# Moving the destination and weight arithmetic of a routed tile ahead in a mixture-of-experts stage, with four-deep buffers for its results

## The reference

```python
logits = jnp.einsum('bsd,de->bse', x, Wr) * SCALE
_, idx = jax.lax.top_k(logits + rb, K)                  # K = 2 of E = 8
w = jax.nn.softmax(jnp.take_along_axis(logits, idx, axis=-1), axis=-1)
...
h = jnp.einsum('bsd,edh->bseh', x, W1) * jax.nn.silu(jnp.einsum('bsd,edh->bseh', x, W3))
expert_out = jnp.einsum('bseh,ehd->bsed', h, W2)        # H = 512
out = jnp.einsum('bsed,bse->bsd', expert_out, w_full)
hs = jnp.einsum('bsd,dh->bsh', x, Ws1) * jax.nn.silu(jnp.einsum('bsd,dh->bsh', x, Ws3))
out = out + jnp.einsum('bsh,hd->bsd', hs, Ws2)
```

## Time and profile before

| | us |
|---|---|
| median of three runs | 3486.91 |
| the profiled execution | 3485.83 |
| its span | 3483.7 |
| shared-expert units, as a stretch | 2744 to 2856 |
| routed units, first and last turn of rows | 2859.5 and 3409.0 |

### The profile page before, as it was taken

One profiled execution on the slowest core, in us unless ns is written; L12 is line 12 of the kernel. 1 busy time (PEld: TensorE's weight loads), 2 busy tenths in 40 slices (PEclk: granted clock), 3 DMA queues, 4 the chain that ended last, 5 costly groups with the idle time before them and its releaser, 6 DMA issues. The chain is left out here.

```text
span 3483.7 us, 52943 instructions
## 1 busy us (share of the span) xinstructions
PE 2999.7 (86%) x17256; PEld 2171.2 (62%) x17256; DVE 2530.5 (73%) x3858; ACT 1449.3 (42%) x2076; POOL 1674.7 (48%) x1186
## 2 busy tenths in 40 slices
PE   6999999698889889889898898988987897777773
PEld 4888888555546545555554554554554897777773
DVE  3555545687897897888888779878877647766666
ACT  2222222354445445445445444544543333333333
POOL 2222222265574565566557556655654343444445
PEclk9999999899999999999999999999998998888886
DMA  8000100200100100100100100100101324444445
GB/s 236 13 14 14 22 18 13 55 25 16 41 25 19 44 19 25 44 13 25 44 18 19 50 13 19 53 15 20 49 13 59 110 71 143 146 144 147 143 138 177
DMA packets 137039, 197.69 MB, mean 57 GB/s; under 512 B 16992, under 2 KB 96864, under 8 KB 136736
## 3 DMA queue, kind: packets, MB, share of 16 engines
q1 hardware_dynamic: 115696, 160.52, 15.7%
q10 hardware_dynamic: 14224, 14.58, 1.6%
q0 software_dynamic: 6816, 18.75, 1.4%
HBM read 118.54 MB, written 41.71 MB: 46 GB/s over the span
## 5 line engine op out<-in xcount | busy, mean ns | idle before, releaser
L1082 ACT ACTIVATE raw<-b_ps 128x1024 f32<-128x1024 f32 x512 | 505.4, 1021 | 460.6 <-PE b_ps L854 385.6
L1226 DVE TENSOR_SCALAR raw<-raw 128x1024 f32<-128x1024 f32 x512 | 578.2, 1135 | 117.5 <-ACT raw L1082 115.5
L965 PE MATMUL b_ps<-raw 128*64 128x512 f32 x2048 | 510.2, 620 | 113.9 <-DVE raw L1226 113.2
L853 PE MATMUL b_ps<-b_QQ,b_KT 128*128 128x512 f32 x1024 | 436.7, 426 | 15.6 <-DMA b_QQ<-b_QQ 8.6
L823 POOL TENSOR_TENSOR b_acc<-b_acc,raw 128x512 f32<-128x512 f32 x256 | 373.0, 1457 | 86.1 <-DVE raw L1226 54.2
L854 PE MATMUL b_ps<-b_QQ,b_KT 128*128 128x512 f32 x1024 | 407.0, 397 | 0.0
L827 POOL TENSOR_TENSOR b_acc<-b_acc,raw 128x512 f32<-128x512 f32 x256 | 388.7, 1518 | 20.1
L806 POOL TENSOR_TENSOR b_QQ<-raw,b_QQ 128x512 fp32r<-128x512 f32 x128 | 165.3, 1291 | 404.5 <-ACT b_QQ L1032 404.5
L1678 PE MATMUL c_ps<-c_xT_l,c_w_h 128*128 128x256 f32 x1504 | 359.1, 322 | 0.0
L965 PEld LDWEIGHTS b_ps<-raw 128*64 128x64 f32 x2048 | 126.3, 138 | 371.2 <-issue 196.8
L853 PEld LDWEIGHTS b_ps<-b_QQ,b_KT 128*128 128x128 f32 x1024 | 195.2, 191 | 247.8 <-issue 188.5
(11 more groups left out here) (262 smaller groups left out, 7268.5 us busy)
## 6 DMA issues: line engine op xcount, KB each, us to landing
c_raw<-in_L_ffn_W_dram SPq DMA_DIRECT2D x117, 512.0 KB, 5.4
b_QQ<-b_QQ SPq DMA_DIRECT2D x128, 256.0 KB, 3.7
xs<-zeros ACTq DMA_DIRECT2D x1, 10140.0 KB, 67.9
c_xg<-xs SPq DMA_DIRECT2D x39, 260.0 KB, 2.7
b_rows<-in_ctx_dram SPq DMA_DIRECT2D x9, 1024.0 KB, 7.5
a_xt<-in_x_dram SPq DMA_DIRECT2D x72, 64.0 KB, 2.2
b_rows<-x SPq DMA_DIRECT2D x9, 512.0 KB, 7.1
x<-a_x1t SPq DMA_DIRECT2D x64, 64.0 KB, 1.9
```

Source lines behind the costliest of these rows:

```text
L853: pe.matmul(bank(key, a), k, QQ[:, n % 2, hh, 0, :], start=True, stop=False)
L965: mm = pe.matmul(bank(key)[hh * HD:(hh + 1) * HD, :], V[:, t, (2 * p + hh) * HD:(2 * p + hh + 1) * HD], probs[:, at_step(j, hh), (t % 2) * ...
L1082: ins = act.activation(probs[:, at_step(j, hh), :], both(key), ACT.Exp, scale=SCALE)
L1226: dve.tensor_scalar(pr, pr, HI, LO, ALU.min, ALU.max).then_inc(clipped, 1)
```

## The change

The instructions of `goals` are issued elsewhere and in other forms:

- In the list of VectorE `goals(u + 1 - DENSE)`, for the next unit, stands behind `lo(u, 0)`; `goals(u - DENSE)` at the end of the unit is gone. SyncE's list is not edited.
- `share` and `goal_u` are four deep. `goals(j)` waits for the sends of tile j - 4, and `take` now waits for the sends of tile j - 2, whose `yr` it overwrites.
- The two `tensor_scalar` instructions become `scalar_tensor_tensor` with a second operand in SBUF, for which there are two new constant tiles, `nought` and `second_at`, that GpSimd fills at the start of the stage. There are eight instructions as before, in another order, with two `link`s in place of three. `goals_ready` is signalled by the one that writes `goal_u`.
- The counts on `consts` go up by two.

```diff
-        share = sb("c_share", [P, 2, 3, TT])
+        share = sb("c_share", [P, 4, 3, TT])
         goal = sb("c_goal", [P, 4, TT])
+        nought = sb("c_nought", [P, TT])
+        second_at = sb("c_second_at", [P, TT])
...
-        goal_u = sb("c_goal_u", [P, 2, TT], U32)
+        goal_u = sb("c_goal_u", [P, 4, TT], U32)
...
+                pool.memset(nought[:, :], 0.0).then_inc(consts, 1)
+                pool.memset(second_at[:, :], float(SECOND)).then_inc(consts, 1)
...
-                            out=ys[:, :], out_offset=bass.IndirectOffsetOnAxis(ap=goal_u[:, j % 2, t:t + 1], axis=0),
+                            out=ys[:, :], out_offset=bass.IndirectOffsetOnAxis(ap=goal_u[:, j % 4, t:t + 1], axis=0),
...
                 def goals(j):
 
-                    k = j % 2
+                    k, q = j % 2, j % 4
                     dve.wait_ge(xg_in[k], 16 * (j // 2 + 1))
-                    if j >= 2:
-                        dve.wait_ge(sent[k], 16 * TT * (j // 2))
+                    if j >= 4:
+                        dve.wait_ge(sent[k], 16 * TT * (j // 2 - 1))
                     own = owner[:, j:j + 1]
-
-                    link(dve.tensor_scalar(goal[:, 2, :], hole[:, :], float(j * T), None, ALU.add))
                     eid, token = xg[:, k, :, EID], xg[:, k, :, TOKEN]
-                    dve.scalar_tensor_tensor(share[:, k, 0, :], eid, own, xg[:, k, :, SHARE], ALU.is_equal, ALU.mult)
-                    dve.scalar_tensor_tensor(share[:, k, 1, :], eid, own, xg[:, k, :, SHARE + 1], ALU.not_equal, ALU.mult)
-                    dve.tensor_scalar(goal[:, 0, :], eid, own, float(SECOND), ALU.not_equal, ALU.mult)
-                    link(dve.scalar_tensor_tensor(goal[:, 1, :], token, 0.0, goal[:, 2, :], ALU.is_equal, ALU.mult))
+
+                    dve.scalar_tensor_tensor(goal[:, 2, :], hole[:, :], float(j * T), nought[:, :], ALU.add, ALU.add)
+                    dve.scalar_tensor_tensor(goal[:, 0, :], eid, own, second_at[:, :], ALU.not_equal, ALU.mult)
+                    dve.scalar_tensor_tensor(share[:, q, 0, :], eid, own, xg[:, k, :, SHARE], ALU.is_equal, ALU.mult)
+                    link(dve.scalar_tensor_tensor(share[:, q, 1, :], eid, own, xg[:, k, :, SHARE + 1], ALU.not_equal, ALU.mult))
+                    dve.scalar_tensor_tensor(goal[:, 1, :], token, 0.0, goal[:, 2, :], ALU.is_equal, ALU.mult)
+                    dve.tensor_tensor(share[:, q, 2, :], share[:, q, 0, :], share[:, q, 1, :], ALU.add)
                     link(dve.tensor_tensor(goal[:, 3, :], goal[:, 0, :], token, ALU.add))
-                    dve.tensor_tensor(goal_u[:, k, :], goal[:, 3, :], goal[:, 1, :], ALU.add)
-                    dve.tensor_tensor(share[:, k, 2, :], share[:, k, 0, :], share[:, k, 1, :], ALU.add).then_inc(goals_ready, 1)
+                    dve.tensor_tensor(goal_u[:, q, :], goal[:, 3, :], goal[:, 1, :], ALU.add).then_inc(goals_ready, 1)
...
                         dve.wait_ge(goals_ready, j + 1)
+                        if j >= 2:
+                            dve.wait_ge(sent[j % 2], 16 * TT * (j // 2))
                         for t in range(TT):
                             ins = dve.tensor_scalar(yr[:, j % 2, t, :], src[:, t * D:(t + 1) * D],
-                                                    share[:, j % 2, 2, t:t + 1], None, ALU.mult)
+                                                    share[:, j % 4, 2, t:t + 1], None, ALU.mult)
...
                     lo(u, 0)
+                    if nxt:
+                        goals(u + 1 - DENSE)
                     if u == 0:
                         places()
                     if u >= DENSE:
                         split_lo(weight_set(u), 2)
                     product(u, 1)
                     lo(u, 1)
-                    if u >= DENSE:
-                        goals(u - DENSE)
```

More of the change, by code:

```diff
@@ L1535, in _ @@
                 pool.memset(every_f[:, :], 1.0).then_inc(consts, 1)
-                pool.wait_ge(consts, 8)
+                pool.wait_ge(consts, 10)
                 pool.tensor_copy(lane[:, :], step_u[:, :]).then_inc(consts, 1)
-                pool.wait_ge(consts, 9)
+                pool.wait_ge(consts, 11)
                 pool.tensor_scalar(steps[:, :], lane[:, :], float(T), None, ALU.mult).then_inc(consts, 1)
@@ L1547, in _ @@
                 pool.tensor_copy(wrs[:, :, 0, :], wr[:, :, :]).then_inc(consts, 1)
-                pool.wait_ge(consts, 16)
+                pool.wait_ge(consts, 18)
                 pool.tensor_tensor(wrs[:, :, 1, :], wr[:, :, :], wrs[:, :, 0, :].bitcast(F32), ALU.subtract
@@ L1616, in logits @@
                     if c == 0:
-                        pe.wait_ge(consts, 17)
+                        pe.wait_ge(consts, 19)
                     else:
@@ L1833, in _ @@
                     link(tops(c))
-                dve.wait_ge(consts, 17)
+                dve.wait_ge(consts, 19)
                 dve.tensor_copy(y[:, :, EID], topi[:, :, 0])
```

## The result

The changed kernel took 3292.59 us (median of four runs, 3288.86 to 3295.84); the kernel before, 3486.72 us on the same chip. The ratio is 0.9443, with a 95% interval of 0.9426 to 0.9459: 194 us less. The profiled execution took 3288.86 us, its span is 3287.0 us. The kernel after is 2 us slower there and the kernel before 7 us faster, so the size of the gain is known to some 10 us.

What follows compares the result with a forecast made beforehand. Row loads waiting for goals bound the routed loop at 14.65 us a turn; VectorE at 9.49 would follow. 37 turns plus 6.7 for add_dense make 357.8 instead of 542.1; with the ends -186.7, so 3300 us, range 3274 to 3352.

Steps and rivals of the forecast that it cites:

- What bounded before: Routed units: the next row load waits for goals, then turn and first product follow; 37 turns of 14.65 us.
- What is late next: Routed units after the change: VectorE's loop sums to 9.49 us a turn, 0.4 above TensorE's 9.07.
- The rule beside it: VectorE instructions with two SBUF inputs contend with GpSimd's SBUF reads; whichever issues first holds the shared pair throughout.
- Rival B: VectorE's L1828 loses the lock to GpSimd's second split: 1.28 us more a turn, +47 us, 3347; chance 0.18 with lower clock.
- add_dense: In eight units, standing ahead of take, it moves the 3.86 us wait by 0.84: 6.7 us in all.
- goals(1): Now issued in unit 16, it costs its 1.1 us once.
- The end: Last unit, lo(53, 1) to the last take: about 9.6 us instead of 13.1, 3.5 less.
- Row loads: SyncE's burst of weights and rows, needing some 5.5 us, comes 13 us ahead of the turn: costed at nothing.
- `sent` in `goals`: goals(j) waits for send(j-4): 8.7 us of room against landings of 5.6 (median) and 8.3 (longest); no wait.
- Rival D: goals(j) waits on VectorE for slow scatters, making it slower: with a landing of 16 us, +81 us, 3568; chance 0.02.
- The clock: TensorE's granted clock in the routed stretch, 0.85 before, would be near 1.0; at 0.85 its 9.07 us would be 10.67.

Runs made afterwards that it cites:

- e3: The kernel before with four row buffers instead of two, goals at the end of the unit in its old forms, results two deep: 3359.5 us.
- e1: The changed kernel with goals back at the end of the unit, new forms and four-deep results kept: 3477.4 us beside 3479.0 for the kernel before.
- e10: The changed kernel with VectorE's split of w3's half, then goals, both between product(u, 1) and lo(u, 1): 3309.09 us, 0.9498 of the kernel before.
- e6: The changed kernel itself, unedited, run again on another chip: 3294.76 us, 0.9464 of the kernel before.
- e4: The changed kernel with share and goal_u three deep instead of four, goals(j) waiting for the sends of tile j-3: 3411.2 us.
- e7: The changed kernel with load_rows(j) waiting for goals(j-1) instead of goals(j-2): 3295.5 us, beside 3294.8 for the changed kernel on the same chip.
- e8: The changed kernel with VectorE's split of w3's half moved from the front of the unit to ahead of product(u, 1): 3285.56 us, 0.9436 of the kernel before.
- e5: The changed kernel with VectorE's split of w3's half moved from the unit's front to between product(u, 1) and lo(u, 1): 3284.55 us, 0.9436 of the kernel before.

## Why the prediction was right

**What bounded before.** e3 shows the row load as a part of the loop worth 3.5 us a turn, e1 that the place of `goals` is what ties it there.

**What is late next.** The sum of VectorE's loop, term by term, from the turn shown above: lo to product 3.89 us (predicted 3.86), product to lo 1.43 (1.39), lo to goals 0.60 (0.61), `goals` 1.02 (1.1), w2 split 1.14 (1.14), product to lo 1.38 (1.39); 9.46 against 9.49. No term is off by more than 0.08, and the errors partly cancel. What made it work is that units 15 and 16 of the kernel before already ran in the order of the new loop, with L1828 between GpSimd's two splits. It got in there in the changed kernel too: in the 36 short forms of L1832 from 2870 us on the mean is 2.07 us. Rival B, the lock lost to the second split, did not occur. It would have needed 3.2.

**The rule beside it.** e1 and e10 bear the rule of the Trainium skill out on its main point ("SBUF — State Buffer", "Who interferes with whom"): an instruction with two SBUF operands that starts during GpSimd's split took 2.26 us on two numbers per partition (0.16 beside no split) and 2.92 on 512 (0.69). On who comes next, when both wait, it leaves the reading open; in this kernel it was VectorE.

**add_dense.** 10.13 - 9.45 = 0.68 us in each of eight units, 5.4 us; I had 0.84 and 6.7. The sum for the 37 turns was 357.8 us, and from `lo(16, 1)` at 2867.65 to `lo(53, 1)` at 3222.80 it took 355.2.

**The small terms.** goals(1) cost 0.7 us (10.11 us from `lo(15, 1)` to `lo(16, 1)`, 9.37 before), not 1.1. The end was forecast 3.5 us shorter and is 3.0. From `lo(53, 1)` to the start of the last `take` it is about 10.2 us, against 13.1 before and 9.6 forecast. Added up, the stage from `lo(15, 1)` on changes by 0.7 - 186.9 - 3.0 = -189.2 us, and the tail behind it by -0.5, against -186.7 in the forecast.

**The rest of the difference.** The forecast was 3300, the median is 3292.6; the profiled execution is 10 us below the forecast for it. 7.05 us of that lie ahead of all that was changed: `lo(15, 1)` starts at 2857.54 in its trace and started at 2864.59 before. Among the experiments whose order up to there is the changed kernel's, it starts at 2859.0 (e6), 2862.3 (e4) and 2864.2 us (e7), and with the old place at 2859.8 (e1). It is scatter of the stages before, and it fell on the side of a larger gain; the prediction did not allow for it. So of the 7.4 us between forecast and median some 3 are terms of the sum, and the rest is luck of the executions and the chip: e6, with a gain of 185 us, is on the other side of the 187 forecast. How late the stage began in the executions that were not profiled isn't known.

**The waits costed at nothing.** Row loads: no wait, as forecast, but the room was mis-sized. From VectorE's split of w2, for which SyncE waits, to the turn of the rows I had 13 us; it is 9.9 (3070.3 to 3080.2), and the row load itself has 7.7 us for a landing of 6.0. So the term of nothing held by 1.7 us, and e7 shows that 4.7 us less would have cost nothing either, since VectorE bounds. `sent` in `goals`: no wait; the room of 8.7 us was counted against a landing of 5.6 to 8.3, but the sends landed in 2.4 to 3.8. Rival D was further away than I put it; e4 shows that its mechanism exists one buffer shallower, and at the price that was worked out for that depth: 12.5 us a turn expected, 12.56 measured.

**The clock.** TensorE's granted clock rose from 0.85 to 1.00 in the routed stretch, with the idle stretches of 3.5 us a turn gone. It is between the two in the kernels that kept a part of them: 0.91 to 0.93 in e4, 0.93 to 0.95 in e3. The gain seems to have needed it: at 0.85 TensorE's 9.07 us would be 10.67 (an estimate, 9.07 / 0.85), more than VectorE's 9.46. No run separates the clock from the change.

## What to carry to other kernels

Free a buffer where its last reader is done, not where that reader's other work happens to stand: eight tiny instructions in the wrong place held a transfer, a transpose and half a product behind them, 3.5 us a turn, and cost 1.7 us more by their stall. When a stage is about to lose its bound, look in the trace for units at its edge that already run without it; here two such units gave the next bound to 0.03 us. On engines that share ports, order by what the other runs at that moment: a subtraction of 0.69 us cost 0.69, 1.38, 2.06 or 2.92 us by its place alone. To be late by a little is the worst place: 0.05 us behind GpSimd's start cost 2.2 us (e10), 0.9 us behind it 1.4 (the changed kernel). And count the room of a transfer to the engine that reads it, not by turns: what looked like 13 us was 9.9.

## What the runs showed of the hardware

- A VectorE instruction with two SBUF operands that waits for GpSimd's split gets in ahead of GpSimd's next one, although that one is ready: GpSimd's pair then takes 4.11 us instead of 3.67.
- An indirect send of 128 rows lands in 2.4 us (median) in the changed kernel, where the second of two starts 1.6 us ahead of the weights' burst of 1.5 MB (3068.70 and 3070.32), and in 5.6 in the kernel before, where both start beside the burst; in e7, with a row load 0.5 us behind the second send, it is 3.4. The sends themselves were not changed.
- GpSimd's send takes 1.80 us (median of 36) when it starts in VectorE's two splits in e8, and 0.96 to 1.00 us where no subtraction of VectorE is running as it starts; that the shared ports are the cause is not shown.
- TensorE's first matmul starts 0.21 us after the end of the VectorE instruction that it waits for (e5 and e8 alike).
